# A fused four-layer kernel on one Trainium2 core: where the first routed experts' results are added, and three orders of TensorE work

## The reference, cut to what matters

```python
x = x + focused_attention(layernorm(x), ctx)
x = x + routed_ffn_0(layernorm(x))
x = x + tanh_attention(layernorm(x), ctx, mask)
x = x + shared_experts(layernorm(x))
x = x + wide_attention(layernorm(x), ctx)
x = x + routed_ffn_2(layernorm(x))
x = x + softmax_attention(layernorm(x), ctx)
x = x + ternary_ffn(layernorm(x))
```

```python
top_v, top_i = jax.lax.top_k(logits, 2)
...
slot = jnp.where(kept, experts * C + pos, E * C)
buf = jnp.zeros((E * C + 1, D), x.dtype).at[slot].set(xf[tokens])
...
ys = yb[jnp.minimum(slot, E * C - 1)] * (weights * kept)[:, None]
out = jnp.zeros((T, D), x.dtype).at[tokens].add(ys)
```

## Time and profile before

| What | Value |
|---|---|
| Time, median of 3 runs | 3054.76 us (3051.03 to 3055.73) |
| The profiled execution's own time | 3083.54 us |
| Its span in the trace | 3081.8 us |
| Mean granted TensorE clock | 0.928 |
| PE busy | 2581.3 us (84%), 15928 instructions |
| PE weight loads busy | 1781.0 us (58%) |
| DVE busy | 1374.2 us (45%), 4831 instructions |
| ACT busy | 1121.8 us (36%), 2609 instructions |
| POOL busy | 824.1 us (27%), 878 instructions |
| DMA | 252.33 MB, mean 82 GB/s |

### The profile page before, as it was taken

How to read it: one execution, slowest core, us unless ns; L and a number is a source line. 1 busy time by engine, 2 the same in 40 slices (tenths; PEclk the granted TensorE clock), 3 DMA queues, 4 the chain that set the end, 5 groups by cost and what they waited for, 6 DMA issues and landing times. The chain is left out here.

```text
span 3081.8 us, 47764 instructions
## 1 busy us (share of the span) xinstructions
PE 2581.3 (84%) x15928; PEld 1781.0 (58%) x15928; DVE 1374.2 (45%) x4831; ACT 1121.8 (36%) x2609; POOL 824.1 (27%) x878
## 2 busy tenths in 40 slices
PE   6998859999938878979999999984999559999586
PEld 4776437777714434547766555663888436666344
DVE  6987502222133444336643333430111357777665
ACT  4554311111118970114444333331333126666321
POOL 3443030000042210007754344503000401212442
PEclk8999879999979998979999999997999769999798
DMA  4232362222022110034210000035777410000000
GB/s 134 84 116 78 146 204 85 84 86 74 14 95 78 60 42 24 0 93 144 111 45 7 11 6 6 1 123 195 293 285 289 140 34 11 10 8 6 28 7 18
DMA packets 69923, 252.33 MB, mean 82 GB/s; under 512 B 16395, under 2 KB 32040, under 8 KB 52264
## 3 DMA queue, kind: packets, MB, share of 16 engines
q1 hardware_dynamic: 60008, 226.24, 20.9%
q0 software_dynamic: 9744, 23.87, 2.5%
HBM read 197.97 MB, written 52.10 MB: 81 GB/s over the span
## 5 line engine op out<-in xcount | busy, mean ns | idle before, releaser
L2597 PE MATMUL L_ffne_up<-L_ffne_xT,L_ffne_wu 128*128 128x128 f32 (+1 forms) x2144 | 391.5, 340 | 33.2 <-DVE L_ffne_xT L2521 23.3
L2597 PEld LDWEIGHTS L_ffne_up<-L_ffne_xT,L_ffne_wu 128*128 128x128 f32 x2144 | 332.2, 194 | 92.9 <-ACT L_ffne_hT L2508 27.5
L1349 PEld LDWEIGHTS L_xattn_pt<-ident,L_xattn_p 112*125 112x125 f32 x1536 | 207.3, 189 | 183.4 <-issue 77.5
L1044 POOL TENSOR_SCALAR L_xattn_p<-L_xattn_p,L_xattn_rec 112x375 f32<-112x375 f32 x256 | 311.6, 1225 | 0.0
L1349 PE MATMUL L_xattn_pt<-ident,L_xattn_p 112*125 112x112 f32 x1536 | 257.7, 289 | 20.9 <-DVE L_xattn_pt L1203 16.0
L1203 DVE COPY L_xattn_pt<-L_xattn_pt 125x336 f32<-125x336 f32 x448 | 216.9, 499 | 125.6 <-PE L_xattn_pt L1349 125.5
L2583 PE MATMUL L_ffne_dn<-L_ffne_wd,L_ffne_hT 128*112 128x256 f32 (+1 forms) x1200 | 266.2, 379 | 1.5 <-issue 1.5
L1186 DVE TENSOR_REDUCE L_xattn_least<-L_xattn_s 112x1 f32<-112x375 f32 x256 | 128.4, 543 | 250.7 <-PE L_xattn_s L1337 250.5
L2583 PEld LDWEIGHTS L_ffne_dn<-L_ffne_wd,L_ffne_hT 128*112 128x112 f32 (+1 forms) x1200 | 216.9, 183 | 39.7 <-issue 2.1
L2484 POOL DMA_DIRECT2D L_ffn_ybuf<-L_ffne_y x75 | 40.1, 534 | 689.1 <-DVE L_ffne_y L2536 405.6
L1127 ACT ACTIVATE L_xattn_p<-L_xattn_ssb,L_xattn_least 112x375 f32<-112x375 f32 x256 | 153.8, 602 | 129.9 <-DVE L_xattn_least L1192 129.0
(11 more groups left out here) (357 smaller groups left out, 4602.2 us busy)
## 6 DMA issues: line engine op xcount, KB each, us to landing
L_ffne_wd<-in_L_ffn_down SPq DMA_DIRECT2D x43, 1024.0 KB, 4.8
L_ffne_wu<-in_L_ffn_up SPq DMA_DIRECT2D x35, 1024.0 KB, 5.4
L_ffne_wu<-in_L_ffn_up SPq DMA_DIRECT2D x8, 2048.0 KB, 7.9
L_xattn_kt<-L_xattn_kd SPq DMA_DIRECT2D x8, 1500.0 KB, 7.7
L_xattn_v<-L_xattn_vd SPq DMA_DIRECT2D x8, 1500.0 KB
L_ffn_xbuf<-L_ffnr_zeros SPq DMA_DIRECT2D x8, 1120.0 KB, 11.8
fa_ctxT<-in_ctxT SPq DMA_DIRECT2D x16, 375.0 KB, 3.6
fa_rows<-in_ctx_rows SPq DMA_DIRECT2D x16, 375.0 KB
```

The source lines that it names most:

```text
L1044: p = pool.tensor_scalar(p_sb[:, head % RP, :], p_sb[:, head % RP, :], rec[:, h, head:head + 1], None, ALU.mult)
L1349: m = pe.transpose(pt_ps[head % 2][0:KP, 0, kt * S:(kt + 1) * S], p_sb[:, head % RP, kt * KP:(kt + 1) * KP], ident[0:S, 0:S])
L2597: m = pe.matmul(up_ps[s % RING][k][:, 0, 0:RH], wu[:, h, c, k * FF + f * 128:k * FF + (f + 1) * 128], xT[:, h, c, q * RH:(q + 1) * RH], st ...
```

## The change

In words. The separate adding stage of the first routed experts goes. `tanh_attention` takes the routing's tables: GpSimd gathers four batches at its start and two more in each of bodies 0 to 5; VectorE adds the first four before the first normalising and two more at the end of each of those bodies. The square root is taken for batches 0 to 3, 4 to 7 and 8 to 15 apart, the second and third within bodies 2 and 6. The batch loops are written out on the engines instead of hardware loops. The output projection of batch b - 2 stands after the transposes in body b (it was that of b - 1 at the body's end), and its residual stands before the next copy.

The first routing hosts batches 4 to 7 (56 parts instead of 42); four parts instead of eight stand ahead of the gap's exponential, in both routings. Values are stored in three pieces, each when its two parts are taken.

In the wide attention, turns from batch 7 on have two score banks and two job banks, a new order of jobs, and both `turn_p` of a pair ahead of the pair's jobs; earlier turns keep three and one. In both expert stages the next block's rows are transposed within the block, one tile after each of up-products 6, 8, 10, 12, 14 in the first, after product 4 in the second.

```diff
-def tanh_attention(core):
+def tanh_attention(core, r):
...
+        RING, OPENING = 4, 4
+        GROUP = (0, OPENING, 2 * OPENING, NB)
+        def arriving(b):
+
+            return range(OPENING + 2 * b, min(OPENING + 2 * b + 2, NB))
...
+                def gather(b):
+                    after(pool, summed, b - RING + 1)
+                    for k in range(2):
+                        pool.indirect_dma_start(
+                            out=got[:, b % RING, k, :], out_offset=None, in_=r.ybuf,
+                            in_offset=bass.IndirectOffsetOnAxis(r.get[:, k, b:b + 1], 0)).then_inc(got_in[b % RING], 16)
+                for b in range(OPENING):
+                    gather(b)
...
+                    for later in arriving(b):
+                        gather(later)
...
-                act.activation(core.std[:, :], mv[:, :, 1], ACT.Sqrt, bias=core.eps[0:S, :]).then_inc(std_done, 1)
+                def deviations(n):
+                    act.wait_ge(stats_done, n + 1)
+                    span = slice(GROUP[n], GROUP[n + 1])
+                    act.activation(core.std[:, span], mv[:, span, 1], ACT.Sqrt,
+                                   bias=core.eps[0:S, :]).then_inc(std_done, 1)
+                deviations(0)
...
+                        if c == 2 and b in (2, 6):
+                            deviations(1 if b == 2 else 2)
...
                 def body(b, h):
-                    if not isinstance(b, int) or b < NB - 1:
+                    if b < NB - 1:
                         normalize(b + 1, 1 - h)
                         take_xt(b + 1, 1 - h)
-                    if not isinstance(b, int) or b > 0:
-                        ch = Chain(dve, chain, (b - 1) * PER)
+                    if b > 1:
+                        residual(b - 2, h, ch)
+                    if b > 0:
                         take_o(b - 1, 1 - h)
                         divide(b - 1, ch)
-                        residual(b - 1, 1 - h, ch)
+                    for later in arriving(b):
+                        add_experts(later)
...
                     if not last:
                         transpose_x(b + 1, 1 - h)
+                    if b > 1:
+                        project(b - 2)
                     scores(b, h, 2)
...
                     products(b, h, 0)
-                    if not first:
-                        project(b - 1)
...
-        slots = [[K[0]], [K[1]], [K[2]], [K[3]], [K[4]], [K[5]], [K[6]], [K[7]], [Q[0]], [Q[1], V[0]],
-                 [Y], [V[1], V[2]], [V[3]], [V[4]], [V[5]], [X]]
+        slots = [[K[0]], [K[1]], [K[2]], [K[3]], [K[4]], [K[5], K[6]], [K[7]], [], [Q[0]], [Q[1]], [Y],
+                 [V[0]], [V[1], V[2]], [V[3]], [V[4], V[5]], [X]]
+        slots_loaded = [[], [], [], [], [], [], [], [], [Q[0]], [Q[1]], [Y], [], [], [], [], [X]]
...
-    NS, NJ = (3, 1) if wide else (4, 1)
+    FREE = 4 if wide else 5
+    SWITCH = FROM - 1 if wide else NB
+
+    def score_banks(b):
+
+        return 2 if wide and b >= SWITCH else FREE - 1
...
-                    after(pe, exp_done if wide else low_done, b * H + pair + 2 - NS)
+                    after(pe, exp_done if wide else low_done, b * H + pair + 2 - score_banks(b))
...
     def store_values(self, sp, b):
-        sp.wait_ge(self.done, (b - self.first + 1) * len(self.parts))
-        sp.dma_start(self.vd[b], self.vs[:, b % 2, :, :]).then_inc(self.v_stored[b % 2], 16)
+        for kt in range(KT):
+            sp.wait_ge(self.done, (b - self.first) * len(self.parts) + self.IC + 2 * kt + 2)
+            sp.dma_start(self.vd[b, :, kt, :], self.vs[:, b % 2, kt, :]).then_inc(self.v_stored[b % 2], 16)
...
-        BESIDE, AHEAD = parts[0:NB], parts[NB:NB + 8]
-        BEHIND = parts[NB + 8:]
+        BESIDE, AHEAD = parts[0:NB], parts[NB:NB + 4]
+        BEHIND = parts[NB + 4:]
...
+        TURN_AT = {(6 + 2 * t if gated else 4): t for t in range(NT)}
...
-                    if not last(b):
-                        turn_rows(b + 1, 1 - h)
+                        if s in TURN_AT and not last(b):
+                            turn_rows(b + 1, 1 - h, TURN_AT[s])
...
-        combine(core, pre, r, not gated, keys)
+        if gated:
+            tanh_attention(core, r)
+        else:
+            combine(core, pre, r, True, keys)
...
-        spilled = SpilledKeysValues(core, "L2_xattn", {"a_": (0, 4), "r_": (4, 7), "c_": (7, 8)})
+        spilled = SpilledKeysValues(core, "L2_xattn", {"a_": (0, 4), "r_": (4, 8)})
```

More of the change, by code:

```diff
@@ L785, in body @@
                 def body(b, h):
-                    first = isinstance(b, int) and b == 0
-                    last = isinstance(b, int) and b == NB - 1
+                    first, last = b == 0, b == NB - 1
                     pe.wait_ge(ctx_in[h], 16 * (b - h) + 32)
@@ L802, in body @@
                     products(b, h, 0)
-                    if not first:
-                        project(b - 1)
                 transpose_x(0, 0)
                 pe.wait_ge(w_in, NLOADS * 16)
-                each_batch(pe, body)
+                for b in range(NB):
+                    body(b, b % 2)
+                project(NB - 2)
                 products(NB - 1, 1, 1)
@@ L900, in softmax_attention @@
         onT = sb("onT", [128, OC, S])
-        job_ps = [core.banks(ctx, f"{n_}job{i}", 1) for i in range(NJ)]
-        s_ps = [core.banks(ctx, f"{n_}s{i}", 1) for i in range(NS)]
+        free_ps = [core.banks(ctx, f"{n_}s{i}", 1) for i in range(FREE)]
         pt_ps = [core.banks(ctx, f"{n_}pt{i}", 1) for i in range(2)]
@@ L971, in projections, with jobs_at @@
                 run("x", 0, -1, 1, 1)
+        def jobs_at(b, head):
+            return (slots_loaded if wide and b < SWITCH else slots)[head]
         def slot_jobs(run, b, h, head, kinds):
-            for kind, i in slots[head]:
+            for kind, i in (jobs_at(b, head) if wide else slots[head]):
                 of = b + OF[kind]
@@ L977, in slot_jobs, with plan, job_bank, wait_bank @@
                     run(kind, i, b, of, (h + OF[kind]) % 2)
+        bank_of, bank_free = {}, {}
+        def plan(kind, i, turn, b, h):
+            first = 2 if wide and turn >= SWITCH else FREE - 1
+            spare = range(first, FREE)
+            at = spare[planned[first] % len(spare)]
+            planned[first] += 1
+            bank_of[kind, i, b] = at
+            if at in last_user:
+                bank_free[kind, i, b] = last_user[at]
+            elif at < FREE - 1:
+                bank_free[kind, i, b] = ("score", SWITCH * H - 1, 0)
+            last_user[at] = (kind, b, i)
+        planned, last_user = {2: 0, FREE - 1: 0}, {}
+        projections(plan)
+        for turn in range(NB):
+            for head in range(H):
+                slot_jobs(plan, turn, turn % 2, head, "kqvxyz")
+        if not wide:
+            plan("z", 0, NB, NB - 1, 1)
+        plan("y", 0, NB, NB - 1, 1)
+        def job_bank(kind, i, b):
+            return free_ps[bank_of[kind, i, b] if wide else FREE - 1]
+        def wait_bank(pe, kind, i, b):
+            if (kind, i, b) in bank_free:
+                was, of, n = bank_free[kind, i, b]
+                if was == "score":
+                    pe.wait_ge(exp_done, of + 1)
+                else:
+                    pe.wait_ge(done[was], made(was, of, n))
         with nc.Block() as block:
@@ L2115, in take @@
         if kind == "v" and part == (0, 0):
[L2116 removed]
+            after(act, self.v_stored[h], before * KT)
         act.wait_ge(self.out, turn + 1)
@@ L2547, in body @@
                     if first(b):
-                        take_rows(0, 0)
+                        for t in range(NT):
+                            take_rows(0, 0, t)
                     for s in range(UPB):
```

152 lines of the change are left out of this document (83 added, 69 removed).

## The result

The changed kernel takes **2966.12 us** (median of 4 runs, 2963.76 to 2966.66) beside 3052.9 before (4 runs): a ratio of 0.9715 (95% interval 0.9698 to 0.9732), 86.8 us less. The forecast was 2953 (2925 to 2986): direction and range held, and the gain was 15 us smaller than its sum of 101.8. The joined part, its first two terms, gave 24 us where they add up to 45; the experts, the wide attention and the second routing gave 10 more than forecast, and the tanh attention cost 4.5 more.

The account below looks back on a forecast made before the run. No one engine was taken to bound the program, so each part was priced in its stage. The terms sum to -101.8 us, 2981.7 by the profiled execution; keeping its 28.8 distance above the median gives 2953 us, range 2925 to 2986.

Parts of the forecast that it names:

- The joined part: Adding stage removed, its projections hosted in the first routing, its adds in the tanh attention; first two terms -66.4 and +21.
- (1): Adding stage of the first experts: it goes entirely, from its first instruction to the tanh stage's first, -66.4 us.
- (2): First routing: hosts the 14 projections; ScalarE's takes stall beside the puts as they did beside gathers, +21 us (bounds 0, +21).
- (3): Both expert stages: row transposes between up-products remove TensorE's waits at block edges, -15 us in the first, -30 in the second.
- (4): Tanh attention: opening +6.2, projection moved -15, adds on VectorE +11, square roots +3.5; together +5.7 us.
- The ring of 14.0: Tanh attention, bodies with adds: dependent steps across engines take 14.0 us against ScalarE's 11.5, +11 us over bodies 1 to 5.
- The opening: Start of the tanh attention: four batches gathered and added first, so first tanh at 19.2 us instead of 13.0, +6.2.
- (5): Wide attention: projecting turns lose 2.0 us each over eight turns, the last turn costs 4; -12 us (bounds -20, 0).
- (6): Second routing: four parts ahead instead of eight, -5.1 us; value stores in three pieces cost 0.
- the hosting was undisturbed: Rival, first routing: hosted takes do not stall although the adding stage's stalls were real, +21 becomes 0; 2932 us, chance 0.20.
- the weights didn't bind: Denies the rival that weight transfers limit the second experts, where -30 becomes -5; 2978 us, chance 0.12.
- two adds beside gathers: Rival, tanh attention: adds beside gathers run at the disturbed 4.9 us instead of 1.7, 32 more; 2985 us, chance 0.12.

Follow-up runs that it names:

- experiments 2 and 10: The changed kernel with stores of values cut into 112 and 13 rows, 2939.82 us, and into 115 and 10 rows, 2966.15 us.
- experiment 6: The changed kernel with the wide attention of the kernel before: 3006.83 us, ratio 0.9744, on the slower chip.
- experiment 7: The changed kernel with both expert stages of the kernel before: 3037.69 us, ratio 0.9848, on the slower chip.
- experiment 3: The changed kernel with the separate adding stage restored, the tanh attention gathering nothing and taking one square root: 2957.41 us, ratio 0.9683.
- experiment 4: The changed kernel with the tanh attention's context loads issued only once the third gathered batch is in: 2966.33 us, ratio 0.9713.
- experiment 11: The changed kernel with each batch's values stored at once, as before, instead of in three pieces: 2958.6 us, ratio 0.968.
- experiments 11 and 9: The changed kernel with each batch's values stored at once, 2958.6 us, and the changed kernel run again unedited, 2963.17 us.
- experiments 1 to 4: Kernel before, profiled again, 3054.05 us; changed kernel with values cut 112/13, 2939.82, adding stage restored, 2957.41, or context loads later, 2966.33.
- 9 to 12: Changed kernel: unedited, 2963.17 us; values cut 115/10, 2966.15; values stored at once, 2958.6; values and context loads cut 112/13, 2942.41.
- experiments 5 to 8: Changed kernel: adding stage restored and values cut 112/13, 2987.32 us; old wide attention, 3006.83; old expert stages, 3037.69; projection at body's end, 3011.47.

## Why the prediction was right, and where it was wrong

**(1) The adding stage, -66.4: it was worth 48.2** (49.0 from the load from which the term counts). I took the profiled execution's own stage, and 17.4 us of it went with the remote waits, which the timed runs of that comparison, by their times, don't have. I had seen this possibility (the 28.8 us between profile and median) and argued that the stalls I booked in (2) cancel it, "the same 2953". That is the step that failed: the cancelling needed (2)'s cost to be stalls, and it wasn't.

**(2) Hosting, +21: it was 23.9, by another cause.** The undisturbed schedule was right to 2 us (first put, last take). The tail was not: I took a third of the 14.0 us store plus a fixed part, 6. In fact the stores were behind by tens of microseconds. The 14.0 us had said it: 1.5 MB in 14 us is 110 GB/s, the rate that the windows show with five of sixteen engines busy. A batch's values need 14 us there, keys and puts come on top, and a batch is taken in 20.4 us. That this is the cause is shown by experiments 2 and 10: the same bytes cut at 112 rows go without a tail, cut at 115 they keep it. The Trainium skill ("DMA: Bandwidth & Descriptors", Why a DMA increments its semaphore by 16 and not by 1) gives the rule: the greatest number of engines up to 16 that divides the outer size, so 5 for 125. The runs agree: share 0.32. With it the tail could have been forecast. That 21 came near 23.9, and that the experts started "near 450" (451.67), was luck: the forecast had stalls in the takes and no tail, the run a tail and no stalls. On the chip that has the remote waits, my mechanism appears as forecast (experiment 6: the last take at 448, not 420), but costs the stage 6 us, not 21.

**(3) Transposes, -15 and -30: -20.3 and -27.1.** Right, and the clearest part (experiment 7). In the second experts the stores of the first and the last block lie 246.3 us apart instead of 276.7, 30.4 less over 34 edges; the stage's opening took 3 of it back. In the first, seven boundaries at 2.4 us are 17; the rest I can't attribute.

**(4) Tanh attention, +5.7: +10.2.** The ring of 14.0 was 13.75 where it closed, in two bodies of the five; adds and square roots together cost 15.5, not 14.5. The projection's move gave its full 15: in experiment 3, which has it without adds, the tanh starts span 181.9 us instead of 198.3. The opening was mis-sized: +10.8, not +6.2. Its term took the first add's delay from a stage without this stage's own loads; here they share the DMA engines (experiment 4 moves it from 9.65 to 7.1), and the expanded queries were waited for whole (1.85), not by half.

**(5) Wide attention, -12: -17.8.** The turns lost nearly their whole slack, 2.66 of the 2.75 of room, where I had granted 2.0; the last turn's price was 2.8, not 4.

**(6) Second routing, -5.1: -6.8.** Right. SyncE's added issues cost nothing in themselves, but the smaller rows cost 11 us of the first routing (experiment 11): the 0 for the three pieces was wrong.

The time stayed within the range because the larger gains of (3), (5) and (6) made up for half of the 21 us that the first two terms lacked; that too is partly luck.

Of the rivals, none came about: the hosting was undisturbed, but late for another reason; the weights didn't bind (301 GB/s); two adds beside gathers took 3.4 us in a body; no remote wait fell into the tanh stage.

## What to carry to other kernels

Before subtracting a stage, ask whether its profile belongs to the runs that are compared: a span 1% above the median is a reason to profile again. A stage that ends in stores should be budgeted by bytes over the rate that the windows show for that very transfer, and a row count such as 125 cut so that its large piece divides by 16: here one line was worth 26 us. Work moved beside other work has to be priced at the cover's end: the joined part cost 8 us alone, and paid only once the store tail was gone.

## What the runs showed of the hardware

- Stores of 125 rows of 4 KB drained at a DMA share of 0.32 and 109 to 112 GB/s, and a store of 128 rows queued with them took 28.5 us to land. Cut into 112 and 13 rows, 0.99 MB of values left in 5 us beside puts, at a share of 0.89, and the keys landed in 6.1 us; cut into 115 and 10, the tail ran at 107 GB/s and 0.35.
- A busy DMA engine stored 26 GB/s with rows of 12 KB and 22 with rows of 4 KB (experiments 11 and 9, worked out from the rows by queue).
- The kernel before took 3053 us beside experiments 1 to 4, 3052 beside 9 to 12, and 3085 beside experiments 5 to 8 (nine runs each). The profiles of the slower chip show waits on "remote" beside long series of indirect transfers, mostly of 2 to 10 us and up to 20 beside the second routing's puts; those of the faster chips show none. What they are stays open, and so does whether the chip makes them or the moment.
- The activation table load took 1.28 us in every row, in the new places too (970.09, 971.71). The Trainium skill ("ScalarE: Activation LUTs", What ACT_TABLE_LOAD costs) makes up its 2.7 of 1.28 for the load and 1.38 for a drain. The load agrees; the drain doesn't show: the activation behind the load at 970.09 starts 1.30 us after it.
